# GNN kernel: the last attention layer's aggregation also normalises and finishes the destinations, and the edge-message stage keeps the source side only

## Chip, cores, metric

One core of a Trainium2 chip runs the whole program. The metric is device microseconds of one execution; the kernel before takes 3662.82 us (median of 3 runs, 3661.37 to 3671.05).

## What is computed

Four graph layers on 50,000 nodes of 128 features with 12,500 edges, each behind a layer norm and ReLU, each added to its input:

```
x = x + L0(h)   # three GAT rounds, one head
x = x + L1(h)   # relational layer, four bases
x = x + L2(h)   # GAT, eight heads of 16
x = x + L3(h)   # edge layer:
  h = features @ W_neigh.T + b_neigh
  h_src = h[src]
  edge_feats = abs(h[dst] - h_src)
  new_h = concatenate([h_src, edge_feats]) @ W_edge.T + b_edge
  seg_sum = segment_sum(new_h, dst);  cnt = segment_sum(ones, dst)
  s = (h + seg_sum) / maximum(cnt, 1)
  z = concatenate([features, s]) @ W_lin.T + b_lin
```

In L3 the reference takes `dst = edge_index[0]`, so its sums run over the nodes that the other layers call sources. A node that is a destination in the other layers only has `z` from its own features; a source node also gets a sum over its edges.

## The kernel before, in words

Nodes that no edge touches go through one long pass (`local_chain`). The nodes at the ends of the edges are held apart in tables of 12,800 rows (`s0`..`s5` for the source end of every edge, `d0`..`d5` for the destination end, sorted by destination). One row of a table is one edge end; a table is worked off in 25 blocks of J = 4 tiles of 128 rows (512 rows, 256 KB). Every layer at the edges is a series of phases, each closed by a barrier of all engines. The engines run their own instruction lists in order and meet at semaphores. Three things set the order in a phase: the list of each engine (steps of a block, each with a lag in blocks), the ring of buffers, and the waits.

The last four phases before the end, with the block `b`:

- **Head projection** (`project` with kind `normed`; tiles `p_`). SP loads both sides of a block into a ring of 7. POOL overwrites source rows that are also destinations, by four gathers from `d4` (L1290), a memset of an idle tile after each. DVE takes mean and variance (`Moments.turn`: `bn_stats`, `bn_aggr`, and the twelve Newton steps for 1/sqrt of the block before). ACT applies them (L1364), PE transposes (L1403), ACT copies with ReLU (L1373), PE multiplies by the 144 columns of weights (L1412, one block later), DVE adds the bias into the held rows (`hold`, L1327, lag 3) and the residual (`residual`, L1340, lag 4). SP stores after the residual of `b` and only then loads block `b + 6`.
- **Attention weights** (`attend`), not touched.
- **Aggregation** (`aggregate`; tiles `c_`). A part that closes sums over tile ends, then per block: SP loads a selection matrix and `d4`, ACT widens the matrix (L1757), PE multiplies it by the held rows (L1787), DVE adds twice (L1715, L1723), SP stores `d5`.
- **Edge messages** (`edge_messages`; tiles `e_`). For both sides of a block: SP loads `s5`, `d5` and keys; POOL gathers over the source rows (L2036); DVE statistics, POOL the power -0.5 (L1111, L1113); DVE and ACT apply; PE transposes 8 tiles; PE and ACT make the features `gt` of both sides (L2176, L2143); PE makes `pz` and `pd` (own part of `z` for source and destination), DVE adds them and a bias row each (L2112, L2114); DVE subtracts the features (L2107), ACT takes the absolute value, PE the message product (L2189, L2190), DVE adds a bias (L2120), PE sums the messages of equal sources inside a tile (L2197), ACT copies the totals (L2155). POOL then adds the totals to a table `acc` in memory by an accumulating scatter (L2055) and writes the finished destinations to the output (L2059), per tile, at lag 3. Each accumulating scatter waits until the one before has landed.

In this phase DVE does every step of a block in one go: statistics, apply, select, combine and messages of the same block. The totals of block `b` need nothing of a later block:

```
stream(eng, (stats, 2), (apply, 2), (index, 0), (select, 2), (combine, 2), (messages, 2))
```

- **Edge outputs** (`edge_outputs`; tiles `o_`): reads `acc`, `gt` and the own part, and scatters the source rows to the output (L2242). Not touched.

## Time and profile before

| | us |
|---|---|
| median of 3 runs | 3662.82 |
| profiled execution, its own time | 3684.87 |
| profiled execution, its span | 3683.2 |
| mean granted TensorE clock | 0.794 |
| busy PE / DVE / ACT / POOL | 2249.8 / 2173.2 / 1669.2 / 2036.5 |

Busy times are sums over a span with many phases, so no engine's share says what a phase waits for. The profiled execution is 22 us longer than the median. The phases that the change touches run one after another from 2535.5 us to the end; a phase begins with the first load that SP issues in it.

The rows below come from two views. The view by stretches has, for each stretch (start:end in us), its length, the busy us of PE, PE's weight loads, DVE, ACT and POOL with their counts, then the granted TensorE clock as a share of 2.4 GHz, the mean busy share of the DMA engines and GB/s. The timeline has start, duration, engine, line, operation, out<-in, count, and in brackets how long the engine sat idle before and what ended that.

### The profile page before, as it was taken

The numbers are of one execution on the slowest core, as the hardware profiler recorded it, in microseconds if no ns is written. First come the engines' busy times: TensorE is split into PE (matmuls) and PEld (weight loads), VectorE is DVE, ScalarE is ACT, GpSimd is POOL, SyncE is SP. The second block draws the span as 40 slices with busy tenths as digits, with TensorE's granted clock in tenths as the row PEclk, the third lists the DMA queues.
The fourth block names the chain that finished last, engine by engine and source line by source line (L and its number), as shares of the span: only waits on it lengthen the run. The fifth ranks groups of instructions, "written<-read, shape, count | busy, mean of one in ns | idle before, by whom it ended". The sixth has DMA issues, their size and how long they took to land. (4 is left out here: it accounts for less than half of the span.)

```text
span 3683.2 us, 52863 instructions
## 1 busy us (share of the span) xinstructions
PE 2249.8 (61%) x12839; PEld 1786.9 (49%) x12839; DVE 2173.2 (59%) x7930; ACT 1669.2 (45%) x3697; POOL 2036.5 (55%) x2221
## 2 busy tenths in 40 slices
PE   2316899998999675446556655874553644545442
PEld 1303666766677564446445553553543533333332
DVE  5516998998999686433534636944558533443242
ACT  0016999999998485222322335832441122222100
POOL 3878765665573431468038336703550058888767
PEclk9998999999999877567757757985666667777665
DMA  2511132332331262754266284425330534343363
GB/s 80 170 41 30 44 98 85 101 99 86 99 98 41 81 181 75 195 131 122 60 183 175 60 229 109 116 82 145 93 79 15 160 90 98 85 99 84 58 184 93
DMA packets 592914, 382.51 MB, mean 104 GB/s; under 512 B 50669, under 2 KB 540622, under 8 KB 592266
## 3 DMA queue, kind: packets, MB, share of 16 engines
q1 hardware_dynamic: 537050, 338.44, 31.5%
q0 software_dynamic: 52800, 39.73, 6.1%
q10 hardware_dynamic: 2800, 1.28, 0.3%
q8 instruction: 109, 1.79, 0.2%
q14 instruction: 155, 1.27, 0.1%
HBM read 250.72 MB, written 153.32 MB: 110 GB/s over the span
## 5 line engine op out<-in xcount | busy, mean ns | idle before, releaser
L1290 POOL DMA_INDIRECT p_a<-t_d,k_map_ix x300 | 312.0, 1040 | 431.8 <-DMA p_a<-t_d 378.0
L830 POOL TENSOR_TENSOR a_rs<-a_ve,w_neg_half 128x16 f32<-128x16 f32 x113 | 330.4, 2924 | 241.7 <-DVE a_ve L766 210.5
L856 ACT ACTIVATE a_nr<-a_xb,a_nm,a_rs 128x128 f32<-128x128 f32 x882 | 371.8, 490 | 26.0 <-POOL a_nm L832 26.0
L1787 PE MATMUL c_pq<-layer_src,c_sel 128*128 (+1 forms) x1000 | 243.1, 421 | 163.4 <-ACT c_sel L1757 107.5
L918 PE MATMUL a_ps<-w_ident,a_nr 128*128 128x128 f32 x1568 | 246.4, 281 | 127.5 <-ACT a_ht L864 47.6
L926 PE MATMUL a_ps<-a_ht,w_aug 128*128 128x512 f32 x588 | 315.0, 621 | 2.3 <-DVE a_ht L733 2.3
L918 PEld LDWEIGHTS a_ps<-w_ident,a_nr 128*128 128x128 f32 x1568 | 180.8, 143 | 276.2 <-issue 243.9
L1787 PEld LDWEIGHTS c_pq<-layer_src,c_sel 128*128 128x128 f32 x1000 | 211.4, 299 | 195.4 <-issue 114.0
L1412 PE MATMUL p_pm<-w_aug,p_ht 128*128 128x130 f32 (+1 forms) x1600 | 290.3, 354 | 8.0 <-issue 3.9
L1412 PEld LDWEIGHTS p_pm<-w_aug,p_ht 128*128 128x128 f32 x1600 | 274.4, 260 | 21.3 <-ACT p_ht L1373 11.2
L733 DVE TENSOR_TENSOR a_ht<-a_ps,a_ht 128x512 f32<-128x512 f32 x294 | 203.0, 694 | 136.2 <-ACT a_ps L871 113.3
L727 DVE BATCH_NORM_STATS2 a_st<-a_xb 128x6 f32<-128x128 f32 x1176 | 253.6, 282 | 0.0
L822 POOL DMA_INDIRECT a_gx<-in_x,a_gi x200 | 204.9, 1025 | 77.0 <-issue 77.0
L864 ACT ACTIVATE a_ht<-a_ps 128x512 f32<-128x512 f32 x392 | 231.3, 590 | 26.9 <-PE a_ps L918 19.5
L2036 POOL DMA_INDIRECT e_a<-t_d,e_ix x100 | 108.6, 1086 | 228.1 <-DMA e_a<-t_s 200.4
L1403 PE MATMUL p_pt<-w_ident,p_a 128*128 128x128 f32 x600 | 110.6, 337 | 201.3 <-DMA p_a<-t_d,k_map_ix 145.6
L1373 ACT ACTIVATE p_ht<-p_pt 128x512 f32<-128x512 f32 x200 | 109.9, 589 | 270.8 <-PE p_pt L1403 136.0
L946 PE MATMUL a_ps<-w_ident,a_bt 128*128 128x128 f32 x784 | 214.7, 274 | 3.3 <-DVE a_xb L791 3.3
L1757 ACT ACTIVATE c_sel<-c_sel 128x512 f32<-128x512 uint8 x125 | 77.9, 630 | 302.7 <-DMA c_sel<-t_sel 174.1
L871 ACT ACTIVATE a_ps<-a_ps,w_b_cols 128x512 f32<-128x512 f32 x294 | 190.1, 649 | 28.1 <-PE a_ps L926 26.0
L1403 PEld LDWEIGHTS p_pt<-w_ident,p_a 128*128 128x128 f32 x600 | 87.4, 175 | 215.7 <-issue 108.2
L856 ACT ACTIVATE a_nr<-a_xa,a_nm,a_rs 128x128 f32<-128x128 f32 x392 | 162.1, 486 | 63.8 <-POOL a_nm L832 59.5
(351 smaller groups left out, 6176.1 us busy)
## 6 DMA issues: line engine op xcount, KB each, us to landing
c_a<-t_d SPq DMA_DIRECT2D x125, 256.0 KB
t_d<-c_a SPq DMA_DIRECT2D x125, 256.0 KB
t_s<-p_a SPq DMA_DIRECT2D x100, 256.0 KB
a_xa<-in_x SPq DMA_DIRECT2D x98, 256.0 KB
out<-a_xb SPq DMA_DIRECT2D x98, 256.0 KB, 2.1
p_a<-t_s SPq DMA_DIRECT2D x75, 256.0 KB
p_a<-t_d SPq DMA_DIRECT2D x75, 256.0 KB
t_acc<-q_zt SPq DMA_DIRECT2D x3, 2171.5 KB
```

The costliest lines, as they stand in the source:

```text
L727: last = v.bn_stats(ST[:, T.at(0, 2), k * J + j, :], rows[:, cols(j)])
L733: v.tensor_tensor(h, PS[ROUND_BANK[k]][:, :], h, ALU.add).then_inc(s_grown[k].sem, 1)
L822: eng.indirect_dma_start(out=GX[:, side, c, :], out_offset=None, in_=x, in_offset=bass.IndirectOffsetOnAxis(ap=GI[:, side, c:c + 1], axis= ...
L830: nc.gpsimd.tensor_tensor(RS[:, z, :], VE[:, z, :], w["neg_half"][:, None, 0:J].to_broadcast([P, LNS, J]), ALU.pow).then_inc(s_rstd.sem, 1)
L856: last = nc.scalar.activation(NR[k][:, T.at(NORM[k], 2), cols(j)], normed_rows(T, k)[:, cols(j)], ACT.Identity, bias=NM[:, T.at(1, SHORT), ...
L864: nc.scalar.activation(HT[k][:, T.at(TURN[k], 2 if k else SHORT), :], PS[TURN_BANK[k]][:, :], ACT.Relu).then_inc(s_relu[k].sem, 1)
L918: last = nc.tensor.transpose(PS[TURN_BANK[k]][:, cols(j)], NR[k][:, T.at(TURN[k], 2), cols(j)], w["ident"][:, :])
L926: nc.tensor.matmul(PS[ROUND_BANK[k]][:, :], w["aug0"][:, k, 0:C], HT[0][:, T.at(ROUND[k], SHORT), :], start=True, stop=True).then_inc(s_pr ...
L946: nc.tensor.matmul(o, BT[:, k - 2, :], w["ident"][:, :], start=True, stop=False, is_transpose=True)
L1290: eng.indirect_dma_start(out=A[:, g, SRC, j, :], out_offset=None, in_=t[f"d{r}"], in_offset=bass.IndirectOffsetOnAxis(ap=k["map_ix"][:, b ...
L1412: last = nc.tensor.matmul(PM[side][:, j, 0:CW], HT[:, b % SHORT, side, cols(j)], rhs, start=True, stop=True)
L1787: last = nc.tensor.matmul(PS[g][:, j, :], SEL[:, g, j, :], keep["src"][:, bass.ds(number(b) * J + j, 1), 0:C].rearrange("p o c -> p (o c)" ...
```

## The change

`project` loses its kind `normed`; the phase is written out as `project_heads`. The bias is now the first of two matmuls into each bank of PSUM, ACT copies the banks to the held rows (`hold`, before the block's `copy`), PE's product comes in the same turn as the transposes, and DVE's residual has lag 3 instead of 4.

`aggregate` is replaced for this layer by `finish_destinations`: beside the aggregation it takes the layer norm of the new destination rows, transposes, makes their features (stored to a new table `gd`) and their own part of `z`, adds, and scatters them to the output, with a memset of an idle tile after each scatter.

`edge_messages` loses the destination side: it loads `gd` ready-made, normalises and transposes 4 tiles, has the Newton steps of `Moments` on DVE in place of POOL's power, the bias `bl_row` as a matmul, and no scatter to the output. Its loops are written out, with these lags. The class `Norms` goes. `Moments.turn` now fits 4 statistics per block as well as 8.

```diff
-def edge_messages(nc, w, k, t, r, out):
+def finish_destinations(nc, w, k, t, r, keep, wm, ws, out):
+    RING, WIDE, SUMS, NORMS = 7, 3, 3, 3
...
+        @block.gpsimd
+            for b in range(BLOCKS):
+                eng.wait_ge(s_od, b + 1)
+                for j in range(J):
+                    m = b * J + j
+                    eng.indirect_dma_start(out=out, out_offset=bass.IndirectOffsetOnAxis(ap=k["out_d_ix"][:, m:m + 1], axis=0),
+                                           in_=OD[:, b % 4, j, :], in_offset=None,
+                                           bounds_check=N - 1, oob_is_err=False).then_inc(s_out[b % 4], 16)
+                    if m:
+                        eng.wait_ge(s_idle, m)
+                    nc.gpsimd.memset(IDLE[:, :], 0.0).then_inc(s_idle, 1)
...
+        @block.vector
+            OUT = 4
+            for n in range(BLOCKS + OUT):
+                if n < BLOCKS:
+                    update(n)
+                if n >= OUT:
+                    output(n - OUT)
+                if n < BLOCKS:
+                    add(n)
+                    eng.wait_ge(s_next, n + 1)
+                if n <= BLOCKS:
+                    mo.turn(eng, lambda m: A[:, n % RING, m, :], n, BLOCKS - 1)
...
+        @block.scalar
+            for n in range(2, BLOCKS + 4):
+                if n < BLOCKS:
+                    widen(n)
+                if 0 <= n - 4:
+                    features(n - 4)
+                if 0 <= n - 2 < BLOCKS:
+                    apply(n - 2)
+                    copy(n - 2)
...
+        @block.tensor
+            for n in range(BLOCKS + 3):
+                if n < BLOCKS:
+                    tiles(n)
+                if 0 <= n - 2 < BLOCKS:
+                    turn(n - 2)
+                if 0 <= n - 3:
+                    product(n - 3)
...
+def edge_messages(nc, w, k, t, r):
+    RING, NORMS, LAG = 7, 4, 4
...
         @block.gpsimd
-            stream(eng, *transfers(0), (lambda b, g: nb.invert(eng, b, g), 1), *transfers(1), *transfers(2), *transfers(3))
...
+            def gather(b, j):
+                m = b * J + j
+                if j == 0:
+                    eng.wait_ge(s_load[b % RING], 16 * uses(b))
+                if b:
+                    eng.wait_ge(s_over[j], 16 * b)
+                eng.indirect_dma_start(out=A[:, b % RING, j, :], out_offset=None, in_=t[f"d{r}"],
+                                       in_offset=bass.IndirectOffsetOnAxis(ap=k["map_ix"][:, m:m + 1], axis=0),
+                                       bounds_check=EP - 1, oob_is_err=False).then_inc(s_over[j], 16)
+            def scatter(b, j):
+                m = b * J + j
+                eng.wait_ge(s_tot, b * 2 + j // 2 + 1)
+                if m:
+                    eng.wait_ge(s_acc, 16 * m)
+                eng.indirect_dma_start(out=t["acc"], out_offset=bass.IndirectOffsetOnAxis(ap=k["acc_ix"][:, m:m + 1], axis=0),
+                                       in_=TOT[:, b % NORMS, j, :], in_offset=None, compute_op=ALU.add).then_inc(s_acc, 16)
+            for n in range(BLOCKS + LAG):
+                for j in range(J):
+                    if n < BLOCKS:
+                        gather(n, j)
+                    if n >= LAG:
+                        scatter(n - LAG, j)
...
         @block.vector
-            stream(eng, (stats, 2), (apply, 2), (index, 0), (select, 2), (combine, 2), (messages, 2))
+            for n in range(BLOCKS + 3):
+                if n < BLOCKS:
+                    there(eng, n)
+                if n <= BLOCKS:
+                    mo.turn(eng, lambda m: A[:, n % RING, m, :], n, BLOCKS - 1)
+                if 0 <= n - 2 < BLOCKS:
+                    combine(n - 2)
+                if n < BLOCKS:
+                    select(n)
+                if 0 <= n - 3:
+                    messages(n - 3)
...
         @block.scalar
-            stream(eng, (apply, 0), (copy, 0), (features, 0), (absolute, 0), (totals, 0))
+            for n in range(BLOCKS + 2):
+                if n < BLOCKS:
+                    apply(n)
+                    copy(n)
+                    features(n)
+                if 0 <= n - 1 < BLOCKS:
+                    absolute(n - 1)
+                if 0 <= n - 2:
+                    totals(n - 2)
...
         @block.tensor
-            stream(eng, (turn, 0), (product, 0), (edges, 0))
+            for n in range(BLOCKS + 2):
+                if n < BLOCKS:
+                    turn(n)
+                    product(n)
+                if 0 <= n - 1 < BLOCKS:
+                    messages(n - 1)
+                if 0 <= n - 2:
+                    totals(n - 2)
```

How the lists of instructions move, at the places that the prediction rests on. The names are the program's tiles; L numbers are lines of the kernel they come from.

POOL in the middle of the message phase before (`e_nb_ve` and `e_nb_rs` are the power for 1/sqrt, `t_acc` the accumulating scatter, `out` the destinations' scatter, `e_a` the gather):

```order
L2036 DMA e_a<-t_d,e_ix 128x128
L85 ISA x2
L2055 DMA t_acc<-e_tot,e_ix 12928x129
L85 REGISTER_ALU
L2059 DMA out<-e_a,e_ix 50000x128
L85 ISA
L1111 TENSOR_TENSOR e_nb_ve<-e_nb_mv,w_ln_eps 128x8
L85 REGISTER_ALU
L1113 TENSOR_TENSOR e_nb_rs<-e_nb_ve,w_neg_half 128x8
L2036 DMA e_a<-t_d,e_ix 128x128
```

POOL after the change, at the turn in which the scatters begin (the names of the waits are those under which the semaphores were first allocated: `a_loaded10` to `13` are `s_over` of the four tiles, `q_eq` is `s_tot`, `q_tl` is `s_acc`):

```order
L2408 DMA e_a<-t_d5,k_map_ix 128x128 [waits a_loaded10,a_squashed2]
L2417 DMA t_acc<-e_tot,k_acc_ix 12928x129 [waits q_eq]
L2408 DMA e_a<-t_d5,k_map_ix 128x128 [waits a_loaded11]
L2417 DMA t_acc<-e_tot,k_acc_ix 12928x129 [waits q_tl,q_eq]
L2408 DMA e_a<-t_d5,k_map_ix 128x128 [waits a_loaded12]
```

The destinations' scatter and the power have left the list; gather and accumulating scatter alternate, and the gather is of the block four ahead of the scatter's. DVE in the message phase before, from the shift of one block to its messages:

```order
L1119 SCALAR_TENSOR_TENSOR e_nb_sh<-e_nb_mv,e_nb_rs 128x8
L1127 TENSOR_SCALAR e_ht<-e_a,e_nb_mv,e_nb_rs 128x128 x4
L2083 TENSOR_SCALAR e_ix<-k_map_ix 128x4
L2083 TENSOR_SCALAR e_ix<-k_acc_ix 128x4
L2083 TENSOR_SCALAR e_ix<-k_out_d_ix 128x4
L2102 TENSOR_TENSOR e_sel<-e_kb,k_src_col 128x512
L2107 TENSOR_TENSOR e_ad<-e_gt 128x512
L2112 TENSOR_TENSOR e_a<-e_a,e_pz 128x512
L2114 TENSOR_TENSOR e_a<-e_a,w_bl_row 128x512
L2112 TENSOR_TENSOR e_a<-e_a,e_pd 128x512
L2114 TENSOR_TENSOR e_a<-e_a,w_b_row 128x512
L2120 TENSOR_TENSOR e_ms<-e_pm,w_be_row 128x4x128
```

and after, from the end of one turn of `Moments` to the start of the next:

```order
L1141 BN_AGGR e_mo_mv<-e_mo_st 128x2
L1115 SCALAR_TENSOR_TENSOR e_mo_sh<-e_mo_mv,e_mo_rs 128x4
L2446 TENSOR_TENSOR e_ad<-e_gt,e_gd 128x512
L2449 TENSOR_TENSOR e_a<-e_a,e_pz 128x512
L2438 TENSOR_TENSOR e_sel<-e_kb,k_src_col 128x512
L2456 TENSOR_TENSOR e_ms<-e_pm,w_be_row 128x4x128
L1130 BN_STATS e_mo_st<-e_a 128x6
L1108 TENSOR_SCALAR e_mo_ve<-e_mo_mv 128x4
```

In turn n, `e_mo_sh` is of block n - 1, `e_ad` of n - 2 and `e_ms` of n - 3, and all of them now stand behind the statistics of block n. DVE in the aggregation had L1715 and L1723 in turn; after the change one block of `finish_destinations` begins so:

```order
L2187 TENSOR_TENSOR c_pq<-c_pq,layer_dst 128x512
L2199 TENSOR_TENSOR c_rows<-c_pq,c_a 128x512
L2193 TENSOR_TENSOR c_a<-c_pq,c_a 128x512
L1130 BN_STATS c_mo_st<-c_a 128x6
L1108 TENSOR_SCALAR c_mo_ve<-c_mo_mv 128x4
L1112 TENSOR_SCALAR c_mo_hf<-c_mo_ve 128x4
L1113 TENSOR_SCALAR c_mo_rs<-c_mo_ve 128x4
```

The output of block n - 4 (`c_rows`) stands between the two additions, and a whole turn of statistics and Newton steps follows them.

## Rows read from the trace of the kernel before

**Rows 1.** Stretches (columns above): relational layer, head projection, aggregation, messages, outputs.
```profile
2280.00:2380.00 100.00, 91.36 (x456) 59.47 (x456) 98.22 (x592) 86.28 (x218) 73.87 (x111) 1.00 0.44 121
2535.53:2778.90 243.37, 127.65 (x600) 113.30 (x600) 134.24 (x802) 104.10 (x251) 134.34 (x200) 0.66 0.33 88
2867.54:2949.53 81.99, 49.42 (x208) 42.71 (x208) 33.35 (x53) 15.45 (x25) 0.00 (x0) 0.61 0.64 182
2949.53:3512.35 562.82, 266.04 (x1300) 190.94 (x1300) 212.12 (x776) 140.58 (x275) 425.01 (x350) 0.69 0.37 84
3512.35:3683.00 170.65, 61.22 (x300) 54.73 (x300) 60.51 (x125) 0.00 (x0) 131.75 (x200) 0.59 0.50 149
```
**Rows 2.** Timeline, POOL, messages: start, us, engine, line, operation, count, [idle before <-releaser].
```profile
3203.59 1.05 POOL L2036 DMA_INDIRECT e_a<-t_d,e_ix  x1 [0.30 <-issue]
3205.03 1.61 POOL L2055 DMA_INDIRECT t_acc<-e_tot,e_ix  x1 [0.39 <-issue]
3206.94 1.03 POOL L2059 DMA_INDIRECT out<-e_a,e_ix  x1 [0.30 <-issue]
...
3210.16 1.09 POOL L2036 DMA_INDIRECT e_a<-t_d,e_ix  x1 [0.20 <-issue]
```
**Rows 3.** Timeline, POOL, end of messages: no gather left in the list.
```profile
3491.95 1.55 POOL L2055 DMA_INDIRECT t_acc<-e_tot,e_ix  x1 [1.27 <-issue]
...
3495.96 1.55 POOL L2055 DMA_INDIRECT t_acc<-e_tot,e_ix  x1 [1.12 <-issue]
...
3500.45 1.55 POOL L2055 DMA_INDIRECT t_acc<-e_tot,e_ix  x1 [1.60 <-issue]
```
**Rows 4.** Timeline, head projection: last gather of a block, first statistics behind it.
```profile
2562.89 1.01 POOL L1290 DMA_INDIRECT p_a<-t_d,k_map_ix  x1 [0.16 <-issue]
2565.57 0.29 DVE L1184 BATCH_NORM_STATS2 p_mo_st<-p_a 128x6 f32<-128x128 f32 x1 [2.90 <-DMA p_a<-t_d,k_map_ix]
...
2752.76 1.01 POOL L1290 DMA_INDIRECT p_a<-t_d,k_map_ix  x1 [0.16 <-issue]
2757.51 0.29 DVE L1184 BATCH_NORM_STATS2 p_mo_st<-p_a 128x6 f32<-128x128 f32 x1 [4.79 <-DMA p_a<-t_d,k_map_ix]
```
**Rows 5.** Timeline, DVE, head projection: stage's first statistics; one turn's two ends.
```profile
2550.37 1.70 DVE L1184 BATCH_NORM_STATS2 p_mo_st<-p_a 128x6 f32<-128x128 f32 x8 [14.29 <-DMA p_a<-t_d,k_map_ix]
...
2650.55 0.29 DVE L1184 BATCH_NORM_STATS2 p_mo_st<-p_a 128x6 f32<-128x128 f32 x1 [4.78 <-DMA p_a<-t_d,k_map_ix]
...
2653.70 0.19 DVE L1169 SCALAR_TENSOR_TENSOR p_mo_sh<-p_mo_mv,p_mo_rs 128x8 f32<-128x8 f32 x1
```
**Rows 6.** Timeline, messages: ACT and PE of one block, and PE to ACT totals.
```profile
2980.45 1.16 PE L2197 MATMUL e_po<-e_ms,e_sel 128*128 128x129 f32 x8 [0.78 <-DVE e_ms L2120]
2981.20 0.83 ACT L2155 ACTIVATE e_tot<-e_po 128x258 f32<-128x258 f32 x2 [3.63 <-PE e_po L2197]
...
3210.40 1.65 ACT L1136 ACTIVATE e_ht<-e_a,e_nb_sh,e_nb_rs 128x128 f32<-128x128 f32 x4 [6.15 <-DVE e_nb_sh L1119]
3211.56 1.97 PE L2168 MATMUL e_pt<-w_ident,e_ht 128*128 128x128 f32 x8 [7.73 <-DVE e_ht L1127]
3212.70 0.60 ACT L2133 ACTIVATE e_ht<-e_pt 128x512 f32<-128x512 f32 x1 [0.65 <-issue]
3213.36 2.07 PE L2176 MATMUL e_pg<-e_ht,w_wnT 128*128 128x512 f32 x2
3216.37 1.10 PE L2176 MATMUL e_pg<-e_ht,w_wnT 128*128 128x512 f32 x2 [0.95 <-ACT e_gt L2143]
```
**Rows 7.** Timeline, PE, head projection: 32 passes of two blocks without a gap.
```profile
2769.65 4.29 PE L1412 MATMUL p_pm<-w_aug,p_ht 128*128 128x144 f32 x32
```
**Rows 8.** Timeline: first update of the aggregation; a scatter with its idle memset.
```profile
2879.64 0.70 DVE L1715 TENSOR_TENSOR c_pq<-c_pq,layer_dst 128x512 f32<-128x512 f32 x1 [7.75 <-PE c_pq L1787]
...
3525.09 1.00 POOL L2242 DMA_INDIRECT out<-o_sz,k_out_s_ix  x1 [21.77 <-DVE o_sz L2270]
...
3526.59 0.99 POOL L2242 DMA_INDIRECT out<-o_sz,k_out_s_ix  x1 [0.17 <-issue]
```

More of the change, by code:

```diff
@@ L1214, in project @@
     CW = C + 2 * heads
[L1215 to L1216 removed]
+    first = kind == "first"
+    norm, overlay = first, not first
     RING, SHORT = 7, 3
@@ new lines, in edge_messages, with there @@
+        s_load, s_gd, s_sz_out = ([sem(f"{n}{g}") for g in range(RING)] for n in ("load", "gd", "sz_out"))
+        s_kb, s_gt_out = ([sem(f"{n}{g}") for g in range(NORMS)] for n in ("kb", "gt_out"))
+        s_over = [sem(f"over{j}") for j in range(J)]
+        block = ctx.enter_context(nc.Block())
+        cols = lambda j: slice(j * C, (j + 1) * C)
+        uses = lambda b: b // RING + 1
+        def there(eng, b):
+            for j in range(J):
+                eng.wait_ge(s_over[j], 16 * (b + 1))
@@ L2191, in edges, with messages @@
+            def messages(b):
+                m = b % NORMS
+                eng.wait_ge(s_abs, b + 1)
+                if b:
+                    eng.wait_ge(s_ms, b)
+                for j in range(J):
+                    nc.tensor.matmul(PM[:, j, :], GD[:, b % RING, cols(j)], w["weT"][:, 0, :], start=True, stop=False)
+                    last = nc.tensor.matmul(PM[:, j, :], AD[:, m, cols(j)], w["weT"][:, 1, :], start=False, stop=True)
                 last.then_inc(s_nh, 1)
-                wait(eng, s_ms, b + 1)
```

669 lines of the change are left out of this document (449 added, 220 removed).

## The prediction

> **What bounds the kernel now.** I read the stretches first, since busy shares over the whole span mix phases with different limits. The three touched phases take 243.4, 82.0 and 562.8 us and the outputs, untouched, 170.7 [rows 1]. In the message stretch the reader should see POOL with 425.0 of 562.8 us busy and no other engine over 266. POOL's timeline there shows why: gather, accumulating scatter and destinations' scatter take 1.35, 1.91 and 1.33 us each with the idle time before them, and that idle time is put down to issuing, not to a wait [rows 2]. So 562.8 / 25 = 22.5 us per block, start and end included, is POOL's own list. The accumulating scatters alone, once no gather is left in between, come every 4.01 us [rows 3] because each waits for the landing of the one before. In the head projection no engine is over 134.3 of 243.4 us, and the granted clock is 0.66 [rows 1]: it is bound by waits. One last gather and the statistics behind it are 2.7 us apart, another pair 4.8 [rows 4]. There the ring matters: the load of block b + 6 waits for the store of b, which waits for a residual four turns late. The aggregation is 82 us for 25 blocks, 3.3 each, DVE 33.4 busy and POOL empty [rows 1]: loads bound it, 182 GB/s.
>
> **Messages: what leaves and what takes its place.** POOL loses 100 destinations' scatters and the power. What is left of a block is 4 gathers of 1.35 and 4 accumulating scatters of 1.91, 13 us of issue, or 4 x 4.01 = 16.0 if the landing sets the pace. That would be faster than 22.5. But the order excerpts show a new wait. POOL issues gather (n, j), then scatter (n - 4, j). The scatter of block b needs the totals of b. ACT's totals of b stand behind apply, copy and features of b + 2, and PE's behind transposes and products of b + 2 and messages of b + 1. Apply of b + 2 needs the shift of b + 2, which DVE computes in its turn b + 3, and that turn first waits for all four gathers of b + 3. The messages of b, too, are in that turn. The last gather of b + 3 is issued one slot before gather (b + 4, 0) and scatter (b, 0). So POOL stands at scatter (b, 0) until the whole chain behind gather (b + 3, 3) is through, and behind it on POOL wait the gathers (b + 4, 1 to 3), on which the next turn of the chain hangs. It is a closed loop, one period per block:
>
> - gather (b + 3, 3) to DVE: 3.0, between 2.7 and 4.8 [rows 4];
> - DVE's turn: 3.5. The old one takes 2653.70 + 0.19 - 2650.55 = 3.3 for 8 statistics [rows 5]; the new one has 4, but an aggregation and twelve Newton steps stay in it; 2.6 to 4.0;
> - ACT applies 4 tiles: 1.65 + 0.2 to hand over = 1.85 [rows 6];
> - PE transposes 4 tiles: half of 1.97 is 0.99, with hand-over 1.14 [rows 6];
> - ACT copy to the end of PE's product for the features: 0.60 + 2.07 = 2.7 at the lower clock, 1.7 at the upper [rows 6];
> - 32 passes of PE (16 for the own part with its bias, 16 for messages): 32 x 0.134 = 4.3 [rows 7], 4.6 with hand-overs, 8.6 at half clock;
> - totals, PE then ACT: 1.2, from 2980.45 to 2981.20 and on, half a block [rows 6].
>
> These make 18.0. On POOL follows, from scatter (b, 0) to gather (b + 4, 3), two periods of scatters (1 and 2 are held by landings) and one issue: 2 x 4.01 + 1.9 = 9.9 [rows 2, 3]. **Period 28** us. With the low ends (2.7, 2.6, and 1.7 for the products) it is 25.8; with the high ends, the turn at 4.0 and the passes at half clock among them, 28 + 1.8 + 0.5 + 4.0 = 34.3.
>
> Start: DVE's first statistics came 14.8 us into the head projection [rows 5]. Gather (3, 3) lands 12 gathers of 1.35 later, and the 15 of the chain behind a landing follow: first scatter at 14.8 + 16.2 + 15 = 46. The last gathers are those of block 24, and scatter (21, 0) is the last that waits behind any, so there are 21 periods of 28: 588. Then the 15 steps to the last scatter at 4.01: 60. End 12, as from 3500.45 to 3512.35 [rows 1, 3]. Sum 46 + 588 + 60 + 12 = 706, against 562.8: **+142**, rounded down. With 25.8 and 34.3 per period: +96 and +275.
>
> The work taken off DVE here (212 busy of 563, never the bound [rows 1]) is worth nothing by itself; the bias as 16 passes of PE is in the 32 above.
>
> **Aggregation becomes finish_destinations.** In place of 3.3 us per block there are now loads, DVE's two additions and output, statistics, ACT and PE work and 4 scatters. POOL: each scatter with its memset 1.50, so 6.0 per block [rows 8]. The loop: shift of block b to apply 1.85, transposes 0.9 to 1.1, features and own part 3.2, ACT in between 0.4, the tiles of the next block 1.1, update and output and add on DVE 0.65 + 0.61 + 0.7 (0.70 for one update [rows 8]), turn 3.5: 13.0 over two blocks, 6.5 each; with PE at the lower clock 8.6. I take 6.8, over POOL's 6.0 because the clock of this stretch was 0.61 [rows 1]. First update at 2879.64 - 2867.54 = 12.1 [rows 1, 8], 24 x 6.8 = 163, then four lags and the last scatters' landing, about 4 x 5.5 + 12 = 34. 209 - 82 = **+127**. Ends: 6.0 gives +108, 8.6 gives +170.
>
> **Head projection.** Same POOL list, 4 x 1.50 = 6.0 per block as the floor [rows 8]. PE needs 8 transposes (1.1 to 2.0 [rows 6]) and 32 passes (4.3 [rows 7]; it was 127.65 / 25 = 5.1 busy per block [rows 1]). The bias moves from DVE to PE, the holding of rows to ACT: 8 applies are 3.3, two copies and two holds at 0.6 another 2.4, so 5.7 [rows 6]. The residual one turn earlier frees the ring one turn earlier. Product, hold and copy follow each other in one turn on one bank: 4.3 + 0.83 + 0.60 and 0.3 to hand over make 6.0 [rows 6, 7]. Today's is (243.4 - 14.8 - 21.4) / 24 = 8.6, the 21.4 from the last statistics at 2757.51 to the end [rows 1, 4, 5]. I take 6.9, a tenth and more above the floor since the stages before it never ran at theirs: 14.8 + 24 x 6.9 + 17 = 197, with one lag less at the end, **-46**. Ends: 6.0 gives -68; PE at half clock through the stretch, with 2 x 5.1 and 0.5 for the bias passes 10.7 per block, gives +45. The relational stretch, with the same shape of work, ran at clock 1.00 with PE 91.4% busy [rows 1], which makes the lower end nearer.
>
> **Outputs** get the same tables: 0. Attention weights: 0. **Sum** 142 + 127 - 46 = +223. The profiled execution took 3684.87 on its own, 22 above the median; all terms are differences inside it, so I add them to the median: 3662.8 + 223 = **3886** (3908 against a profiled execution like this one).
>
> How long one accumulating scatter of 128 x 129 floats, 66 KB, holds the next enters the period twice and the tail 15 times. In POOL's tail they are 4.01 us apart, with POOL busy 1.55 of it and idle before each [rows 3], and that is what I use. The Trainium skill, "DMA: Bandwidth & Descriptors", section "Anatomy of one DMA — SWDGE (gpsimd) path", fits one such transfer with about 2.0 us plus its bytes over 436 GB/s, which an estimate of mine makes 2.15 here. By that the landing would be over before POOL has issued gather and scatter in the loop, 1.35 + 1.91 = 3.26 apart, so the period would be 1.5 shorter, and the tail 28: 21 x 1.5 + 28 = 60 us less, 3826. The trace disagrees, with 4.01, and the sum goes by the trace.
>
> **Rivals.**
>
> A, above: 0.78.
>
> B, faster. Four blocks of lag are enough, the scatter never waits for its totals, and the phase is bound by the chain of accumulating scatters, 4.01 each [rows 3]: 46 + 100 x 4.01 + 12 = 459, -104. Total 3662.8 - 104 + 127 - 46 = 3640. For it: POOL at 425 of 563 busy is by far the most loaded [rows 1], and the destinations' scatter leaves it for a phase in which POOL did nothing. It decides when the chain of 18 fits into the gap between gather (b + 3, 3) and scatter (b, 0), which is one scatter and one gather, some 6 us. By every row above it doesn't. 0.10, for a mistake of mine in which turn holds what. The Trainium skill's "Perfetto Trace Analysis", section "Identifying the Most-Contended Engine", says to find the most occupied engine and optimise it first; that is this rival, and the occupancy agrees with it, at 425 of 563 us.
>
> C, worse. PE's clock stays at its lower level, 1.2 GHz, through messages, as the outputs stretch had 0.59 with PE busy 61 of 171 us [rows 1]. The period grows by the 32 passes again, 4.3, and a second time the transposes, 1: 33.3, and 21 x 5.3 = 111 over A, 3997. The more POOL waits, the less PE does. 0.08.
>
> D, no change in messages. More of the chain overlaps than I see, DVE's turn runs at 2.6, the period is 21 to 23, messages about 560: 3662.8 + 0 + 127 - 46 = 3744. 0.04.
>
> **Numbers.** Forecast 3886. All low ends together (period 25.8, +108, -68) give 3662.8 + 96 + 108 - 68 = 3799; I set the lower end at 3795. The upper, 3975, has the period at 31 (+63) and 26 for the other two terms, whose high ends are 43 and 91 off. That leaves out B, D and most of C. Runs of before spread from 3661.37 to 3671.05, so 0.3% (11 us) is about what can be told from no change. Slower 0.89 (A, C, D, 0.90 together, less 0.01 in case D falls together with the low end of the head projection), same 0.01 for that, faster 0.10 (B).
>
> **What would show it.** Right: in messages, POOL's first accumulating scatter of each block waits about 12 us for ACT's totals and these waits are 28 apart; DVE waits for gathers; the stretch is about 706 with POOL under 350 busy. finish_destinations about 209, POOL near 150 busy, DVE waiting for PE's tiles. Head projection about 197 at a higher clock. Wrong: the accumulating scatters come every 4.0 from first to last with no wait for totals (B); a period of 28 with another releaser than the totals; or finish_destinations hidden so well that it ends near 110.

## The result, and the profile after

The changed kernel takes 3850.7 us (median of 4 runs, 3845.87 to 3852.82) against 3662.1: a ratio of 1.0511, with an interval of 1.0487 to 1.0535. 188.6 us were lost; the forecast was 223 (3886 us), and the range of 3795 to 3975 holds the time. One execution of the kernel with lag 5 (below) took 4877 us and is left out of its time; it is the one that was profiled, so no stretch of that kernel is shown.

First the stretches of the changed kernel: head projection, finish_destinations (with the 3 us in which the last closing sums are stored ahead of it), messages, outputs. The columns are those of [rows 1].

```profile
2519.60:2701.70 182.10, 133.97 (x1000) 125.59 (x1001) 102.07 (x752) 131.08 (x301) 134.89 (x200) 0.90 0.44 118
2787.00:2983.70 196.70, 112.08 (x758) 93.69 (x758) 121.89 (x608) 84.08 (x175) 130.94 (x200) 0.85 0.46 140
2983.70:3678.20 694.50, 214.89 (x1150) 176.35 (x1150) 132.18 (x626) 105.26 (x225) 262.46 (x200) 0.63 0.29 59
3678.20:3850.90 172.70, 60.09 (x300) 53.76 (x300) 61.23 (x125) 0.00 (x0) 133.89 (x200) 0.61 0.50 148
```

| stretch | before, us | after, us | difference | forecast |
|---|---|---|---|---|
| head projection | 243.4 | 182.1 | -61 | -46 |
| aggregation, then finish_destinations (both with the 3 us) | 84.9 | 196.7 | +112 | +127 |
| messages | 562.8 | 694.5 | +132 | +142 |
| outputs | 170.7 | 172.7 | +2 | 0 |

The four differences add up to 184 us, near the 188.6 between the medians. The two profiled executions are only 3852.82 - 3684.87 = 168 us apart: phases ahead of these, which the change doesn't touch, took 16 us less in the second trace (the head projection begins at 2519.6 and not at 2535.5). So the total can't be checked against the terms to better than some 20 us, and the stretches are the finer test.

In messages PE, DVE, ACT and POOL all work less than before [rows 1], POOL by 163 us, and the stretch is 132 us longer. No share of busy time says why; the accumulating scatter does. First what POOL sat idle for ahead of all 100 of them, in the view of that one source line (us, times; 22 of the 24 are first scatters of a block); then POOL's timeline in the middle.

```profile
  ACT e_tot L2505: 274.6, 24
  DMA t_acc<-e_tot,k_acc_ix: 103.6, 72
```
```profile
3302.80 1.59 POOL L2417 DMA_INDIRECT t_acc<-e_tot,k_acc_ix  x1 [12.34 <-ACT e_tot L2505]
...
3313.16 1.04 POOL L2408 DMA_INDIRECT e_a<-t_d,k_map_ix  x1 [0.30 <-issue]
3315.44 1.59 POOL L2417 DMA_INDIRECT t_acc<-e_tot,k_acc_ix  x1 [1.24 <-DMA t_acc<-e_tot,k_acc_ix]
3317.33 1.04 POOL L2408 DMA_INDIRECT e_a<-t_d,k_map_ix  x1 [0.30 <-issue]
3329.96 1.59 POOL L2417 DMA_INDIRECT t_acc<-e_tot,k_acc_ix  x1 [11.59 <-ACT e_tot L2505]
...
3340.19 1.04 POOL L2408 DMA_INDIRECT e_a<-t_d,k_map_ix  x1 [0.30 <-issue]
```

Once per block POOL stands 12 us on ACT's totals; 3302.80 to 3329.96 is one period, 27.2 us. In [rows 2] the same instruction waited for nothing but its issue. What happens in the 16.8 us between the gather at 3313.16 and the release at 3329.96 is the loop that the prediction walked through (timeline of the same stretch, all engines):

```profile
3315.78 0.29 DVE L1130 BATCH_NORM_STATS2 e_mo_st<-e_a 128x6 f32<-128x128 f32 x1 [22.29 <-DMA e_a<-t_d,k_map_ix]
...
3318.46 0.16 DVE L1115 SCALAR_TENSOR_TENSOR e_mo_sh<-e_mo_mv,e_mo_rs 128x4 f32<-128x4 f32 x1
...
3318.65 1.65 ACT L2478 ACTIVATE e_ht<-e_a,e_mo_sh,e_mo_rs 128x128 f32<-128x128 f32 x4 [15.86 <-DVE e_mo_sh L1115]
...
3320.35 1.11 PE L2526 MATMUL e_pt<-w_ident,e_ht 128*128 128x128 f32 x4 [18.15 <-ACT e_ht L2478]
...
3321.50 0.60 ACT L2484 ACTIVATE e_ht<-e_pt 128x512 f32<-128x512 f32 x1 [1.20 <-PE e_pt L2526]
...
3322.15 2.07 PE L2534 MATMUL e_pg<-e_ht,w_wnT 128*128 128x512 f32 x2 [0.69 <-ACT e_ht L2484]
...
3328.59 1.06 PE L2559 MATMUL e_po<-e_ms,e_sel 128*128 128x129 f32 x8
3329.30 0.77 ACT L2505 ACTIVATE e_tot<-e_po 128x258 f32<-128x258 f32 x2 [3.74 <-PE e_po L2559]
```

Every wait in brackets ends with the step before it: DVE was idle for 22 us until the gather, ACT 16 until the shift, PE 18 until ACT. All four engines wait for one another in turn, and POOL's part (3329.96 to 3340.19, 10.2 us) closes the circle.

### The profile page after: what moved, and what is told of

It reads as the page before. It is cut to its first block and busy times, and to the rows that moved or that the text cites. A ratio compares the mean times of both kernels' runs of the same rounds, so it can differ in the third digit from the quotient of the medians.

```text
span 3850.9 us, 53130 instructions
## 1 busy us (share of the span) xinstructions
PE 2255.6 (59%) x13639; PEld 1824.4 (47%) x13639; DVE 2144.5 (56%) x8280; ACT 1726.8 (45%) x3847; POOL 2001.2 (52%) x2271
## 5 line engine op out<-in xcount | busy, mean ns | idle before, releaser
L2417 POOL DMA_INDIRECT t_acc<-e_tot,k_acc_ix x100 | 158.5, 1585 | 385.3 <-ACT e_tot L2505 274.6
L1236 POOL DMA_INDIRECT p_a<-t_d,k_map_ix x200 | 207.9, 1040 | 201.1 <-DMA p_a<-t_d 166.5
L1130 DVE BATCH_NORM_STATS2 e_mo_st<-e_a 128x6 f32<-128x128 f32 x100 | 28.7, 289 | 479.7 <-DMA e_a<-t_d,k_map_ix 479.7
L2526 PE MATMUL e_pt<-w_ident,e_ht 128*128 128x128 f32 x100 | 26.8, 420 | 437.5 <-ACT e_ht L2478 437.5
L1884 PE MATMUL c_pq<-layer_src,c_sel 128*128 (+1 forms) x800 | 194.2, 420 | 142.8 <-ACT c_sel L1854 110.0
L1884 PEld LDWEIGHTS c_pq<-layer_src,c_sel 128*128 128x128 f32 x800 | 168.7, 298 | 168.5 <-issue 90.9
L2526 PEld LDWEIGHTS e_pt<-w_ident,e_ht 128*128 128x128 f32 x100 | 17.5, 211 | 441.8 <-ACT e_ht L2478 382.5
L2478 ACT ACTIVATE e_ht<-e_a,e_mo_sh,e_mo_rs 128x128 f32<-128x128 f32 x100 | 41.2, 482 | 390.4 <-DVE e_mo_sh L1115 390.4
L1352 PE MATMUL p_pm<-w_aug,p_ht 128*128 128x130 f32 x1200 | 201.0, 336 | 7.2 <-ACT p_ht L1314 6.7
L1314 ACT ACTIVATE p_ht<-p_pt 128x512 f32<-128x512 f32 x150 | 83.2, 590 | 264.8 <-PE p_pt L1343 264.5
```

Source lines behind the costliest of these rows:

```text
L1236: eng.indirect_dma_start(out=A[:, g, SRC, j, :], out_offset=None, in_=t[f"d{r}"], in_offset=bass.IndirectOffsetOnAxis(ap=k["map_ix"][:, b ...
L1352: last = nc.tensor.matmul(PM[side][:, j, 0:CW], HT[:, b % SHORT, side, cols(j)], rhs, start=True, stop=True)
L1884: last = nc.tensor.matmul(PS[g][:, j, :], SEL[:, g, j, :], keep["src"][:, bass.ds(number(b) * J + j, 1), 0:C].rearrange("p o c -> p (o c)" ...
```

## The experiments

All phases end in barriers, so a kernel may carry two edits in two phases, and each is read from its own stretch. The message phase came first: is it the lag, and which list holds the totals?

**Lag 5 in place of 4.**

```diff
-    RING, NORMS, LAG = 7, 4, 4
+    RING, NORMS, LAG = 7, 4, 5
```

> Only change against the changed kernel: POOL's scatter of the message phase is five blocks behind its gather, not four (LAG 4 to 5). Theory (closed loop: scatter (b, 0) waits for totals that stand behind the turn of block b + 3, and holds the gathers of b + 4): the scatter now has a whole further turn of POOL between gather (b + 3, 3) and itself, about 20 us against the chain of 16.8 that the changed kernel's trace shows (gather at 3313.16, scatter released at 3329.96). No wait for totals is left but at the start; the landings set the pace, 4.15 us each: 44.3 + 100 x 4.15 + 11 = 470 us for the phase in place of 694.5, total 3851 - 224 = 3626, which is below the kernel before. Rival 1 (the phase is slow because PE's clock fell to its lower level): the lag changes nothing there, 3851. Rival 2 (the ring of source rows holds the gathers next: a load waits for a store of the block seven back): some of it, between 20 and 24 us a block, 3700 to 3790.

Measured: 3731.5 us, ratio to the kernel before 1.0168 (1.0146 to 1.0190), where the changed kernel has 1.0511. One number takes away two thirds of the loss: the lag is its cause, and rival 1 falls. But 3626 wasn't reached. The time lies in the range of rival 2, yet its mechanism is not there: in the traces of lag 6 and of lag 5 with half of the loads (both below) only the phase's first gather waits for a load. What holds the pace instead, the kernels below show.

**The lists reordered, lag 4 kept.** In three kernels the steps of older blocks go first, on DVE alone, on ACT and PE alone, and on all three. On DVE for instance:

```diff
             for n in range(BLOCKS + 3):
-                if n < BLOCKS:
-                    there(eng, n)
-                if n <= BLOCKS:
-                    mo.turn(eng, lambda m: A[:, n % RING, m, :], n, BLOCKS - 1)
                 if 0 <= n - 2 < BLOCKS:
                     combine(n - 2)
-                if n < BLOCKS:
-                    select(n)
                 if 0 <= n - 3:
                     messages(n - 3)
+                if n < BLOCKS:
+                    select(n)
+                    there(eng, n)
+                if n <= BLOCKS:
+                    mo.turn(eng, lambda m: A[:, n % RING, m, :], n, BLOCKS - 1)
```

> Against the changed kernel, lag 4 kept: in the message phase ACT does absolute and totals of the older blocks before apply, copy and features of the new one, PE messages and totals before transposes and product. DVE as it was. Theory: the totals of b then no longer stand behind the new block's work on ACT and PE, but still behind DVE's turn of b + 3, because the subtraction for b + 1 and the messages of b come after it. The chain behind the last gather loses apply, transposes, copy, features product and own part: statistics 2.6 later, shift 2.7 after that, then subtract 0.7, absolute 0.65, 16 passes 2.1, totals 1.2: released about 10.3 us after the gather, not 16.8. Period 27.2 - 6.5 = 20.7, total 3851 - 21 x 6.5 = 3714. Rival (the order on ACT and PE is not what holds the totals): 3851.

> Against the changed kernel, lag 4 kept: in the message phase DVE does combine, messages and select before it waits for the gathers of the new block and takes its statistics. ACT and PE as they were. Theory: totals of b still stand on ACT and PE behind apply, transposes and products of b + 2, which need the turn of b + 3 and its gathers; the chain is untouched, since DVE's steps were beside it. No change: 3851, within 0.3%. Rival (DVE's wait for the gathers in front of the messages is the cause): the period falls by several us, under 3750.

> Against the changed kernel, lag 4 kept: both reorderings together, older blocks' steps first on DVE, ACT and PE. Theory: the totals of b now need nothing later than the gathers of b + 2. The chain behind those is longer, about 5.3 to the shift, 6.6 to the features, then 0.7 + 0.65 + 2.1 + 1.2, some 16.6 us, but POOL needs about 19 us from gather (b + 2, 3) to scatter (b, 0) at the pace of the landings. So the waits vanish as with the larger lag: phase about 470, total about 3626. Neither reordering alone reaches that. Rival: the gains of the two parts only add, about 3714.

Measured: ACT and PE alone 3822.5 (ratio 1.0411, 1.0382 to 1.0440), DVE alone 3941.6 (1.0735, 1.0709 to 1.0762), all 3737.1 (1.0179, 1.0151 to 1.0206). In the traces of this group the head projection and finish_destinations, which the edits don't touch, take some 40 to 46 us more than in the first trace (the control, below), so the totals show less of a gain than the message stretches do. These, in that order:

```profile
3040.40:3652.00 611.60, 257.85 (x1150) 216.39 (x1150) 132.16 (x626) 105.52 (x225) 262.16 (x200) 0.64 0.33 68
```
```profile
3030.70:3766.00 735.30, 224.37 (x1150) 183.36 (x1150) 136.94 (x626) 105.44 (x225) 262.93 (x200) 0.62 0.27 56
```
```profile
3043.10:3566.70 523.60, 223.26 (x1150) 179.26 (x1150) 133.06 (x626) 108.09 (x225) 264.67 (x200) 0.70 0.38 79
```

What holds the totals is as the theory has it: with one list reordered the totals still wait for a later block, with all of them they don't, and 694.5 becomes 523.6 at the same lag. All three sizes were wrong, for three reasons: PE's clock, SP's transfers and a wait of DVE.

ACT and PE first gained 83 us in the stretch, not 136. The chain lost the steps it should, but PE, idle for 10.7 us before the message products, now does them at its lower clock: the granted clock from 3314.41 to 3317.90 is 0.50. PE's timeline there:

```profile
3314.41 0.77 PE L2548 MATMUL e_pm<-w_weT,e_gd 128*128 128x128 f32 x2 [10.67 <-DVE e_ms L2456]
...
3317.52 0.64 PE L2549 MATMUL e_pm<-w_weT,e_ad 128*128 128x128 f32 x2
3317.95 1.93 PE L2559 MATMUL e_po<-e_ms,e_sel 128*128 128x129 f32 x8
```

16 passes take 3.5 us from start to start, and the totals' products 1.93. In the changed kernel it is 1.8 (3326.80 to 3328.59) and 1.06: there PE has done the features and the own part just before, the first of it at 0.50, and the granted clock is 1.00 from 3326.10 on. The two differences are 2.6 us per period, and 21 x 2.6 = 55 us is about the gain that is missing (136 - 83 = 53).

DVE first, forecast at no change, lost 41 us in the stretch, and "all first" stopped at 18.8 us a block on average and not 16.6. The second, and about 24 of the 41, have the same cause. In "all first", the timeline of SP, ACT's totals and POOL:

```profile
3214.97 0.37 SPq L2390 DMA_DIRECT2D t_sz<-e_a  x1
3215.39 0.50 SPq L2379 DMA_DIRECT2D e_kb<-t_src_row  x1
...
3215.54 2.07 POOL L2417 DMA_INDIRECT t_acc<-e_tot,k_acc_ix  x1 [1.09 <-DMA t_acc<-e_tot,k_acc_ix]
3215.93 0.44 SPq L2371 DMA_DIRECT2D e_a<-t_s  x1
3216.42 0.54 SPq L2374 DMA_DIRECT2D e_gd<-t_gd  x1
...
3218.26 0.77 ACT L2504 ACTIVATE e_tot<-e_po 128x258 f32<-128x258 f32 x2 [5.14 <-PE e_po L2558]
...
3222.79 1.59 POOL L2417 DMA_INDIRECT t_acc<-e_tot,k_acc_ix  x1 [3.83 <-DMA t_acc<-e_tot,k_acc_ix]
```

SP issues four transfers of 256 KB in 2 us, and the scatter issued among them holds the next for 7.25 us from start to start, not 4.1. It isn't totals that the next waits for: ACT made those of its own block at 3198.27, and those shown, at 3218.26, are already the next block's.

The same trace has a stretch to compare with. SP's last load is issued at 3414; up to there a block takes 18.8 to 21.3 us, with one landing in each that is 6.2 to 7.8 us from start to start, and behind it 16.2 to 17.8.

In the changed kernel the same four transfers go out at 3319.88 to 3321.34, in the middle of POOL's 12 us of waiting, and delay nothing. With DVE first they moved to just ahead of the scatter: there SP's last is at 3324.36. POOL's scatters behind it, and a step of DVE near the start of that kernel's phase:

```profile
3325.14 1.59 POOL L2417 DMA_INDIRECT t_acc<-e_tot,k_acc_ix  x1 [11.94 <-ACT e_tot L2504]
...
3331.46 1.59 POOL L2417 DMA_INDIRECT t_acc<-e_tot,k_acc_ix  x1 [3.38 <-issue]
```
```profile
3059.80 0.69 DVE L2446 TENSOR_TENSOR e_ad<-e_gt,e_gd 128x512 f32<-128x512 f32 x1 [6.43 <-ACT e_gt L2491]
```

The 6.32 us between the two scatters are the most; the other gaps of this kind are 4.8 to 6.0, and the 21 periods together are 24 us longer than in the changed kernel. The other 18 of the 41 us are at the start: the first scatter comes 62.5 us into the phase and not 44.3, since DVE now waits for features of an older block, here 6.4 us, before it takes the statistics of the next. The expectation had that wait at nothing.

**Lag 5, and half of the burst left out.**

```diff
-                    eng.wait_ge(s_nh, b - RING + 1)
+                    return
                 eng.dma_start(GD[:, g, :], t["gd"][b * P:(b + 1) * P, :]).then_inc(s_gd[g], 16)
...
-                    eng.wait_ge(s_sel, b - NORMS + 1)
+                    return
```

> The message phase with lag 5, and after the first blocks SP loads neither the keys nor the destinations' features any more (the selection and the subtraction use old data; half of SP's 1 MB burst per block is gone). Theory: with lag 5 and with all steps reordered the phase took about 20.0 us a block and not 16.6, because one landing in each block comes 3 to 4 us late, just when SP has issued four transfers of 256 KB (at 3214.97 to 3216.96 in the reordered one, scatter at 3215.54, next only at 3222.79). With half the burst that landing is about half as late: 18.2 us a block, the phase 45 us shorter than with lag 5. Rival 1 (the lateness is in the accumulation itself, some rows of the table take longer): no change. Rival 2 (any collision costs the whole): no change either, but the late landing would then be seen behind the two transfers left.

The selection and the subtraction then work on old data. Measured: 3692.6 (1.0064, 1.0046 to 1.0083), 39 us less than lag 5. Its message stretch, its scatters with the two transfers that are left, and the first and last start of all 100:

```profile
3010.80:3511.10 500.30, 214.24 (x1150) 175.17 (x1150) 132.31 (x626) 104.99 (x225) 263.89 (x200) 0.67 0.33 62
```
```profile
3202.95 0.36 SPq L2390 DMA_DIRECT2D t_sz<-e_a  x1
3203.15 1.84 POOL L2417 DMA_INDIRECT t_acc<-e_tot,k_acc_ix  x1 [2.06 <-issue]
3203.36 0.51 SPq L2371 DMA_DIRECT2D e_a<-t_s  x1
...
3209.30 1.59 POOL L2417 DMA_INDIRECT t_acc<-e_tot,k_acc_ix  x1 [2.96 <-DMA t_acc<-e_tot,k_acc_ix]
```
```profile
L2417 POOL DMA_INDIRECT t_acc<-e_tot,k_acc_ix x100: 1550/1591/2106, 3059.2 to 3500.8; - x100
```

(3500.8 - 3059.2) x 4 / 99 = 17.8 us a block, against 18.8 with the whole burst (lag 6, below): 25 us in 25 blocks; the two stretches differ by 33, as lag 6 also starts its scatters 9 us later. The forecast gain of 45 came as 39 in the totals. The late landing of a block is now 4.9 to 6.8 us from start to start, against 6.3 to 8.1 with lag 6, and the rows added are the same: the collision, not the table's rows, makes it late. How the burst does it, by the engines or by the memory, no run here takes apart.

**What the moved scatters could bring at best, and what they cost.** The remaining kernels take the phases of before and of the change apart. The changed kernel again, then the new head projection alone in the kernel before:

> The changed kernel again, untouched, as the reference of this group. In the four kernels run before, head projection and finish_destinations, which none of them touches, took 202 to 208 and 216 to 217 us; in the first trace of the changed kernel 182 and 194. If that belongs to the chip, this one shows the same here, about 3850 + 45 = 3890; if to the run, its phases vary within this group.

> The kernel before with the new head projection alone in it (written out, bias as a matmul, residual lag 3); aggregation and messages as before. Theory (the terms add, since a barrier closes each phase): 243 us become 182 to 207, so 36 to 61 us faster than the kernel before. Rival (the gain needs the other parts of the change): within 0.3% of before.

Measured: control 3878.1 (1.0580, 1.0554 to 1.0607); head projection alone 3625.3 (0.9877, 0.9853 to 0.9902). The latter beats both kernels, by 1.2% against the kernel before. The control is 27 us above the first measurement of the same kernel. The stretches of the control (heads, finish, messages), and the head projection in the other:

```profile
2522.70:2712.40 189.70, 136.04 (x1000) 129.61 (x1000) 100.70 (x752) 132.77 (x300) 134.95 (x200) 0.89 0.42 114
2798.20:3011.10 212.90, 123.93 (x758) 100.47 (x758) 121.01 (x608) 84.09 (x176) 130.65 (x200) 0.84 0.42 129
3011.10:3700.10 689.00, 211.49 (x1150) 172.34 (x1150) 132.07 (x626) 105.22 (x225) 262.58 (x200) 0.63 0.29 60
```
```profile
2520.70:2720.30 199.60, 138.51 (x1000) 132.05 (x1001) 101.11 (x752) 132.98 (x301) 134.34 (x200) 0.87 0.40 108
```

The head projection takes 182 to 208 us from one trace to the next with the same code, finish_destinations 197 to 217; the message phase 689 to 695. In the 182 POOL's gathers follow one another with no wait over 0.6 us (1.49 each with the memset, 1.52 on average, 6.1 a block, where the prediction's floor was 6.0); in the slower ones POOL waits for a load in some blocks, up to 2.2 us in the control and up to 5.4 in those of the group before. The new phase differs in three things (bias as a matmul, ACT's copy to the held rows, the residual one turn earlier), and no run takes them apart.

**A ring of 8 in the head projection; no memsets in finish_destinations.**

```diff
-    RING, SHORT = 7, 3
+    RING, SHORT = 8, 3
...
-                    if m:
-                        eng.wait_ge(s_idle, m)
-                    nc.gpsimd.memset(IDLE[:, :], 0.0).then_inc(s_idle, 1)
```

> The changed kernel with two edits in two phases apart: head projection with a ring of 8 blocks in place of 7, and finish_destinations without the memset of an idle tile after each scatter. Head projection: where it takes 207 us, POOL waits 2 to 4.5 us for loads in each block; theory: one more block in the ring takes that away, so 182 as in the first trace; rival: it stays at 207, the loads are late for another reason. finish_destinations: theory: it is bound by POOL's list, 1.47 us per scatter and memset; without the memset 1.33, and DVE's 5.3 per block is the next bound, so 14 us less than the control; rival: PE or DVE bound it and it stays.

Measured: 3883.0 (1.0584, 1.0556 to 1.0612), head projection 194.8 us and finish_destinations 214.5, against 189.7 and 212.9 of the control. Neither edit does anything that stands out of the spread between traces. With the ring of 8 POOL waits for a load only once by more than 0.6 us (1.3 us; five times in the control, 0.9 to 2.2), but its gathers take 157 us from first to last against 160, and behind the last of them come 33 us and not 25. So late loads are not what sets this phase, and POOL's list isn't what binds finish_destinations there.

**finish_destinations without its scatters; messages with lag 6.** The scatters and the waits for them are left out, so the destinations' rows of the output are missing.

> The changed kernel with two edits in two phases apart: messages with lag 6, and finish_destinations without its scatters (rows of the output missing). Messages: theory: with lag 5 no wait for totals was left, so lag 6 gives the same, about 520 to 530 us for the phase; rival: one more turn of slack takes up the late landings, under 500. finish_destinations: the run without memsets left it at 214 us against 213, so it is not POOL's list alone that binds; theory: the chain over DVE, ACT and PE takes 6 us a block itself, so without any scatter it still takes 185 to 200; the tail of scatters after the last block, 20 to 30 us, is all that goes. Rival (the scatters bind it): 82 us as the aggregation before plus little, 120 to 150.

Measured: 3668.8 (0.9998, 0.9975 to 1.0022). The two stretches, the 100 accumulating scatters, and DVE's first step of three blocks:

```profile
2800.70:2964.00 163.30, 113.96 (x758) 95.01 (x758) 119.18 (x608) 84.06 (x175) 0.00 (x0) 0.91 0.45 133
2964.00:3497.00 533.00, 213.47 (x1150) 175.20 (x1150) 132.14 (x626) 104.80 (x225) 260.72 (x200) 0.66 0.38 77
```
```profile
L2404 POOL DMA_INDIRECT t_acc<-e_tot,k_acc_ix x100: 1542/1579/1613, 3021.1 to 3486.3; - x100
```
```profile
2869.39 0.70 DVE L2176 TENSOR_TENSOR c_pq<-c_pq,layer_dst 128x512 f32<-128x512 f32 x1 [1.12 <-PE c_pq L2276]
...
2874.24 0.70 DVE L2176 TENSOR_TENSOR c_pq<-c_pq,layer_dst 128x512 f32<-128x512 f32 x1
...
2880.08 0.70 DVE L2176 TENSOR_TENSOR c_pq<-c_pq,layer_dst 128x512 f32<-128x512 f32 x1 [1.12 <-PE c_pq L2276]
```

Lag 6 is no better than lag 5: (3486.3 - 3021.1) x 4 / 99 = 18.8 us a block. Without scatters finish_destinations takes 163 us, below my 185: a chain over two blocks of 10.7 us (2869.39 to 2880.08), as the prediction drew it, but 5.35 a block and not 6.5. Of the 112 to 128 us that the phase grew by, 78 are thus the norm, features and additions (163.3 - 84.9). The other 33 in the first trace are the end alone: from first to last update DVE takes 5.27 us a block with the scatters and 5.23 without, but POOL's list still runs when DVE is done. The other 50 of the control are 21 of such an end and 27 of a slower chain, 6.37 a block. Whether the scatters slow the chain there isn't shown: the first trace has them at 5.27.

**The kernel before, with POOL relieved in two ways.** On top of the new head projection: the power on DVE; the destinations' scatters left out (those rows of the output missing); both.

```diff
-            stream(eng, *transfers(0), (lambda b, g: nb.invert(eng, b, g), 1), *transfers(1), *transfers(2), *transfers(3))
+            stream(eng, *transfers(0), *transfers(1), *transfers(2), *transfers(3))
...
-            stream(eng, (stats, 2), (apply, 2), (index, 0), (select, 2), (combine, 2), (messages, 2))
+            stream(eng, (stats, 2), (lambda b, g: nb.invert(eng, b, g), 2), (apply, 2), (index, 0), (select, 2), (combine, 2), (messages, 2))
```
```diff
-                    wait(eng, s_d, (b + 1) * 2)
-                    carry_waits(eng, w)
-                    eng.indirect_dma_start(out=out, out_offset=bass.IndirectOffsetOnAxis(ap=IX[:, g, OUT, j:j + 1], axis=0),
-                                           in_=A[:, g, DST, j, :], in_offset=None,
-                                           bounds_check=N - 1, oob_is_err=False).then_inc(s_out[g], 16)
```

> The kernel before with the new head projection, and in its message phase the power -0.5 taken off POOL: twelve small steps of DVE in its place. Nothing is moved between phases. The trace of before gives 19.4 us a block there at best and 20.6 on average from the first to the last accumulating scatter; lag 5 in the changed kernel gives 18.7 on average. Theory (POOL's list is the bound in the message phase of before, and the landings are just under it): POOL loses about 2 us a block, of which the landings leave 1 to 1.5, so 25 to 40 us off the 3625 of the new head projection alone: 3585 to 3600, faster than both kernels. Rival (the phase is bound by landings already, or DVE's 2.4 us of dependent steps in its one-go turn are as bad): 3625 or above.

> The kernel before with the new head projection, and the 100 scatters of the destinations in the message phase left out (their rows of the output are then missing). This is what moving them could bring at best to this phase. Theory: POOL's list falls by 4 x 1.33 = 5.3 us a block, but the landings of the accumulating scatters do not follow: 16.6 by themselves, 18.7 with SP's bursts, against 20.6: 2 us a block, some 45 us, total about 3580. Rival (POOL's issue time is the whole bound): 5.3 us a block, 130 us, total about 3495.

> Both edits together: no power and no destinations' scatter on POOL, so its list is 13 us a block, as in the changed kernel, with the latency loop of before (lag 3, all of a block's steps in one go). Theory (landings bound it): no faster than the one without the destinations' scatters, within 15 us, about 3575. Rival (POOL's list still counts): 2 us a block more, about 3530.

Measured: 3601.1 (0.9798, 0.9770 to 0.9825), 3586.8 (0.9756, 0.9726 to 0.9786) and 3572.7 (0.9717, 0.9678 to 0.9757). Their message stretches, in that order:

```profile
2883.20:3424.00 540.80, 268.12 (x1300) 193.00 (x1300) 263.54 (x1076) 140.33 (x275) 375.72 (x300) 0.70 0.39 87
```
```profile
2888.40:3418.20 529.80, 266.88 (x1300) 192.85 (x1300) 210.85 (x776) 140.40 (x275) 317.26 (x250) 0.70 0.37 78
```
```profile
2883.70:3389.50 505.80, 252.67 (x1300) 182.72 (x1300) 259.27 (x1076) 140.33 (x275) 268.76 (x200) 0.74 0.39 82
```

Against 562.0 for the phase in the kernel with the new head projection alone, leaving out the 100 scatters wholly, 133 us of POOL's time at 1.33 each, gives 32 us: where POOL no longer fills the time, it waits for landings. In that trace 50 of the 100 accumulating scatters wait for the one before, 86.5 us in all, and in the kernel with the new head projection alone none does. The power off POOL gives 21 us by itself, a little under the 25 to 40 forecast, and 24 more on top of the other edit, which is between the theory's 15 and the rival's 45; in the totals that step is 14 us with overlapping intervals. So POOL's issue time still counts a little below the pace of the landings, and how it does stays open. The kernel with the power on DVE computes everything, and at 3601.1 it is the fastest complete one here, 1.7% below the kernel before by the near end of its interval.

## Why the prediction was right, step by step

**Messages, +142 forecast, +132 measured.** The mechanism, the place and the releaser were as written: the first scatter of each block waits 12 us (11.4 to 12.8, after the first) on ACT's totals, 27.1 to 27.9 apart, 27.4 in the mean, and not 28; the last of the 21 periods is 29.5. By terms: gather to statistics 2.6 (3.0 forecast), turn to ACT's start 2.9 (3.5: with 4 statistics the Newton steps set its length, and they are quicker than I took them), apply 1.7 (1.85), transposes 1.15 (1.14), copy to the end of the features' product 2.7 (2.7, at the lower clock as chosen), the rest with 32 passes and totals 5.7 (5.8), together 16.8; POOL's part 10.2 (9.9). The landings are mostly 4.0 to 4.3 apart; 4.01 was the lowest of the tail of before, whose other gap in [rows 3] is 4.49 and whose ten are 4.14 in the mean. The first scatter came at 44.3 us (46), there were 21 periods, then 62.6 us (60) and an end of 10.5 (12). The forecast's own sum is 706 - 562.8 = 143. The experiments show it to be cause and not company: two more blocks of lag, or the lists reordered with the lag kept, take away the waits and 156 to 171 us of this phase (689.0 or 694.5 to 533.0 or 523.6).

**One transfer's length.** The landings in the changed kernel are mostly 4.0 to 4.3 us apart, 1.6 of it POOL's issue, and in the kernels without the wait 7 where SP's burst falls in. The 2.15 us that the prediction worked out from the Trainium skill's "DMA: Bandwidth & Descriptors", section "Anatomy of one DMA — SWDGE (gpsimd) path", would be near only if it counts from the end of the issue; as it was used there, from the start, the measurement decides against it.

**finish_destinations, +127 forecast, +112 and +128 measured.** Near as a sum, mis-sized in its parts, and the nearness is in part luck. The step "13.0 over two blocks, 6.5 each" was 10.7 and 5.35: I had added DVE's update, output and addition to the turn in full, at the clock of the old stretch (0.61), where this one ran at 0.91 (0.85 with the scatters). The 163 us of "24 x 6.8" came as 126 in the first trace and 153 in the control, and the 34 us behind the last update as 52 and 42. In the first trace POOL's list at 1.47 per scatter trails the chain and runs 21 us past the last output. In the control DVE stands for 2.3 to 4.1 us before every second update, eleven times. For seven of these the trace names a transfer that belongs to no tile of this phase, for four PE's product of the same block, which in one of them had ended 1.4 us before by the trace's estimate (2912.50 + 1.06, update at 2914.98). The other traces of 211 to 217 us have the same stands, the one of 197 and the one without scatters have none. So what DVE waits for stays open, as does why loads are late in the head projection in some traces. Neither stall was tried by itself.

**Head projection, -46 forecast, -61 in the first trace, -54 to -35 in the others.** The term was 6.9 a block; the first trace came to 6.1, next to POOL's floor of 6.0, with the granted clock at 0.90 and not 0.66. The low end of -68 was nearer for that trace, the forecast for the rest.

**Rival B** (four blocks of lag are enough, 3640) was rightly set at little: the chain of 16.8 doesn't fit into 6 us. But its number was wrong too. I took 4.01 a scatter as the pace of a phase without the wait, and repeated that as 3626 in the expectation for lag 5. The kernel with that wait gone takes 3731.5. The missing term is SP's burst, some 3 us in each block that still has loads: the tail of [rows 3], from which the 4.01 was read, has none beside it. POOL was by far the most occupied engine, 425 of 562.8 us [rows 1], and taking 133 us off it is worth 32. The rule of the Trainium skill that the rival rested on ("Perfetto Trace Analysis", section "Identifying the Most-Contended Engine") names the right engine here, but not how far one gets with it.

## What to carry to other kernels

Where one queue issues both the first step of a block and the last step of an older one, count the lag from the lists of all engines: the older block's result may stand behind work for the newest one on any of them, and then a lag that looks ample is a closed loop. Removing issue time from a busy engine gains only down to its next bound (here 32 us out of 133, with half of the scatters then waiting for the landing of the one before), so measure that bound with the work left out before paying for a new home for it. And take the duration of a transfer from a stretch with the same traffic beside it.

## What the hardware showed that I had not expected

A burst of four 256 KB transfers costs a dependent scatter about 3 us when they are issued together (7.25 us from start to start against 4.1) and nothing when they fall into a wait; so shortening one wait moved the burst onto the scatter, and in a reordering that should have been neutral it cost some 24 us. And PE at a granted clock of 0.50 after 10.7 us without work made 16 passes take 3.5 us and not 1.8, and the totals' products 1.93 and not 1.06: the wait for one engine made another slower.
